# A transformer-like block on one core: three side banks and two maximum banks in PSUM, side work placed by free TensorE time

## The reference

```python
x = x + attn_a(ln(x))   # scores = -|pos_i - pos_j| * scale, causal softmax, 16 heads share it; out @ wo.T + bo
x = x + ffn(ln(x))      # sigmoid(xr W_r) * (relu(xk W_k)**2 W_v), xr and xk mix a token with the one before
x = x + attn_b(ln(x))   # 16 heads of 16 channels, softmax(q k / 4), causal
x = x + ffn(ln(x))      # the same weights as the first one
```

## Time and profile before

| what | us |
|---|---|
| three runs, median (lowest to highest) | 2311.16 (2307.39 to 2319.46) |
| the profiled execution's own time | 2316.06 |
| its span, first to last instruction | 2314.3 |
| PE busy (share of the span) | 1929.1 (83%) |
| DVE busy | 1417.5 (61%) |
| ACT busy | 1254.3 (54%) |
| POOL busy | 1024.2 (44%) |

### The profile page before, as it was taken

The page is one execution under the profiler, slowest core; times in us unless marked ns, Lnnn a source line. Parts: engine busy times, 40 slices in busy tenths (PEclk is TensorE's granted clock), DMA queues, the critical chain, the costliest instruction groups (busy, mean ns, idle before and its releaser), DMA issues. The chain is left out here.

```text
span 2314.3 us, 32515 instructions
## 1 busy us (share of the span) xinstructions
PE 1929.1 (83%) x9842; PEld 936.3 (40%) x9842; DVE 1417.5 (61%) x4173; ACT 1254.3 (54%) x2673; POOL 1024.2 (44%) x1074
## 2 busy tenths in 40 slices
PE   4477888888988899788987889888887889988986
PEld 3344343334433354324543345333443335432423
DVE  2336677567676666666765666756656666677642
ACT  0623654675537555394545755366554855555563
POOL 4454354335642455334743266423654246422414
PEclk8677899989998899989999899998999899999998
DMA  3006011310132111211122011231113111141100
GB/s 96 0 20 117 1 28 42 69 28 15 43 85 34 28 29 53 67 29 28 33 67 64 13 29 37 76 63 28 28 37 83 28 28 28 43 87 29 29 19 19
DMA packets 64347, 97.27 MB, mean 42 GB/s; under 512 B 15655, under 2 KB 58029, under 8 KB 58030
## 3 DMA queue, kind: packets, MB, share of 16 engines
q1 hardware_dynamic: 64174, 95.20, 18.6%
HBM read 61.09 MB, written 33.55 MB: 41 GB/s over the span
## 5 line engine op out<-in xcount | busy, mean ns | idle before, releaser
L852 ACT ACTIVATE pt<-exp_bank 128x512 f32<-128x512 f32 (+3 forms) x1536 | 742.5, 494 | 806.5 <-PE exp_bank L822 797.0
L867 DVE CUSTOM_DVE_ANT_0 max_bank<-max_bank,mask 128x128 f32<-128x128 f32 (+3 forms) x1024 | 500.3, 502 | 495.2 <-PE max_bank L811 478.2
L822 PE MATMUL exp_bank<-qs,ks 98*128 98x512 bf16 (+3 forms) x1536 | 523.8, 347 | 72.5 <-ACT pt L852 66.3
L811 PE MATMUL max_bank<-ks,qs 96*128 96x512 bf16 (+3 forms) x1536 | 525.0, 349 | 24.3 <-DVE piece_max L870 17.2
L870 DVE TENSOR_REDUCE piece_max<-max_bank 128x1 f32<-128x512 f32 x512 | 342.9, 686 | 164.7 <-PE max_bank L811 161.5
L837 PE MATMUL o_bank<-pt,v 128*17 128x512 f32 (+3 forms) x3072 | 346.2, 525 | 8.0 <-ACT pt L852 3.0
L889 POOL TENSOR_SCALAR_AFFINE_SELECT pt<-pt 128x512 f32<-128x512 f32 x256 | 170.1, 664 | 404.2 <-ACT pt L852 403.8
L353 POOL TENSOR_SCALAR xh<-xs,mv,rstd 128x256 f32<-128x256 f32 x256 | 322.6, 1266 | 10.0 <-PE side L379 3.8
L822 PEld LDWEIGHTS exp_bank<-qs,ks 98*128 98x128 bf16 x1536 | 153.9, 101 | 353.4 <-ACT pt L852 229.5
L811 PEld LDWEIGHTS max_bank<-ks,qs 96*128 96x128 bf16 x1536 | 154.7, 101 | 257.9 <-issue 102.1
L544 PE MATMUL side<-vp,p 128*128 128x260 f32 x576 | 185.2, 450 | 33.7 <-ACT p L473 18.3
(11 more groups left out here) (94 smaller groups left out, 2243.0 us busy)
## 6 DMA issues: line engine op xcount, KB each, us to landing
parts_dram<-parts SPq DMA_DIRECT2D x64, 384.0 KB, 2.6
qs<-parts_dram SPq DMA_DIRECT2D x192, 128.0 KB, 7.0
ks<-parts_dram SPq DMA_DIRECT2D x32, 384.0 KB, 4.8
xs<-in_L_attn_a_x_dram SPq DMA_DIRECT2D x16, 512.0 KB, 4.3
ks<-parts_dram SPq DMA_DIRECT2D x32, 256.0 KB, 5.5
out_dram<-xs SPq DMA_DIRECT2D x16, 512.0 KB, 3.1
ks<-parts_dram SPq DMA_DIRECT2D x32, 128.0 KB, 5.9
qs<-neg_maxT SPq DMA_DIRECT2D x64, 8.0 KB, 1.9
```

Source lines behind the costliest of these rows:

```text
L811: pe.matmul(max_bank[u % MAX_BANKS][:, 0:k1 - k0], qs[r][0:KROWS, j, P * tile:P * (tile + 1)], ks[r][0:KROWS, j, k0:k1], start=True, stop= ...
L822: pe.matmul(exp_bank[k % EXP_BANKS][:, 0:q1 - q0], ks[r][:, j, P * kt:P * (kt + 1)], qs[r][:, j, q0:q1], start=True, stop=True).then_inc(s ...
L852: act.activation(pt[:, e % 2, j, 0:q1 - q0], exp_bank[k % EXP_BANKS][:, 0:q1 - q0], ACT.Exp, scale=SCALE).then_inc(exp_done, 1)
L867: dve.tensor_tensor_reduce(scores, scores, mask[:, HALF - w:HALF], 1.0, LOWEST, ALU.add, ALU.max, piece_max[:, j, m:m + 1]).then_inc(max_f ...
```

## The change

Eight PSUM banks are divided anew: `side` gets three, `max_bank` two, `exp_bank` keeps two, `o_bank` one. `place()` no longer counts in quarters but in **ticks**. A tick is one side part. `LEFT[u]` is what 2700 columns of PE time leave when the attention of quarter u has had its own (300 at least); the ticks of a group's 48 quarters are shared out in proportion to it, so that 48 ticks still span 48 quarters. `moment(tick)` turns a tick into a quarter with a fraction; the fraction keeps several ticks in one quarter in order, and `schedule()` lists side steps by it. Worked through for the 12 pieces of a group, a quarter gets between 1.06 and 1.46 ticks where it has no products with v, and between 0.19 and 0.65 where it has them (0.19 where both matmuls and the products are at or near 512 columns). The starts, lags and due times of the stages are changed as well, and the long functions of the first attention on PE, DVE and ACT are cut into several generators, so that their steps may be listed interleaved (their semaphores stay as they were). The set-up at the start still uses two side banks in turn.

```diff
-MAX_BANKS, EXP_BANKS = 3, 2
+MAX_BANKS, EXP_BANKS = 2, 2
...
-ATT1, FFN2, FFN4, PROJ3 = -44, 50, 82, 114
-FIRST = {("att1", 0): -220, ("ffn2", 0): -126, ("proj3", 0): -74,
-         ("att1", 1): -28, ("ffn2", 1): 66, ("proj3", 1): 114}
+ATT1, FFN2, FFN4, PROJ3 = -46, 35, 75, 112
+FIRST = {("att1", 0): -240, ("ffn2", 0): -154, ("proj3", 0): -88,
+         ("att1", 1): -36, ("ffn2", 1): 50, ("proj3", 1): 112}
...
-LN_HALF = {"att1": 8, "ffn2": 16, "ffn4": 16, "proj3": 12}
+LN_HALF = {"att1": 12, "ffn2": 20, "ffn4": 20, "proj3": 10}
...
-PIECE_TIME = [2 + (q1 - q0) // P for _, q0, q1 in KEY_PIECES] + [5, 5, 5]
-PIECE_AT = [34 + sum(PIECE_TIME[:p]) for p in range(NP + 4)]
+PIECE_TIME = [max(3, 1 + 5 * (q1 - q0) // HALF) for _, q0, q1 in KEY_PIECES] + [5, 5, 5]
+PIECE_AT = [32 + sum(PIECE_TIME[:p]) for p in range(NP + 4)]
...
-        "att1": [("values1", t, 16 + t + TPH * (t // TPH), 1, 1, 2) for t in range(NT)] +
-                [("positions", k, 29 + k, 1, 1, 1) for k in range(6)] +
+        "att1": [("values1", t, 16 + 2 * t + TPH * (t // TPH), 1, 1, 2) for t in range(NT)] +
+                [("positions", k, 26 + k + 7 * (k // 3), 1, 1, 1) for k in range(6)] +
...
-        "ffn": [("keys", j, 24 + 2 * j, 2, 1, 1) for j in range(2)] +
-               [("receptance", j, 31 + 2 * j, 2, 1, 1) for j in range(2)] +
-               [("products", j, 36 + 2 * j, 2, 1, 2) for j in range(2)],
-        "proj3": [("project", j, 24 + 3 * j, 2, 1, 1) for j in range(8)] +
-                 [("values3", j, 26 + 6 * j, 2, 3, 2) for j in range(4)]}
+        "ffn": [("keys", j, 24 + 3 * j, 2, 1, 1) for j in range(2)] +
+               [("receptance", j, 30 + 4 * j, 2, 1, 1) for j in range(2)] +
+               [("products", j, 37 + 3 * j, 2, 1, 2) for j in range(2)],
+        "proj3": [("project", j, 24 + 4 * j, 2, 1, 1) for j in range(8)] +
+                 [("values3", j, 26 + 4 * j, 2, 1, 2) for j in range(4)]}
...
+def attention_time(u):
+    t, j = divmod(u, GH)
+    width = [k1 - k0 for _, k0, k1 in QUERY_PIECES][t % NP] + [q1 - q0 for _, q0, q1 in KEY_PIECES][(t - LEAD) % NP]
+    return width + (4 * ([q1 - q0 for _, q0, q1 in KEY_PIECES][(t - LEAD - 1) % NP] + 64) if j == GH - 1 else 0)
+
+LEFT = [max(2700 - attention_time(u), 300) for u in range(GH * NP)]
+TICK = [0]
+for u in range(QUARTERS + 200):
+    TICK.append(TICK[-1] + LEFT[u % (GH * NP)] * GH * NP / sum(LEFT))
...
-    free, before, shift, u = [BEGIN, BEGIN], BEGIN, 0, BEGIN
+    free, before, shift, tick = [BEGIN, BEGIN, BEGIN], BEGIN, 0, BEGIN
...
-        side = [psum(f"side{k}") for k in range(2)]
+        side = [psum(f"side{k}") for k in range(3)]
...
-                for entry in parts:
-                    while entry[0] <= u:
-                        entry[0] = next(entry[1], NEVER)
-                parts = [entry for entry in parts if entry[0] < NEVER]
+                while parts and (first := min(parts, key=lambda entry: entry[0]))[0] < u + 1:
+                    first[0] = max(first[0], next(first[1], NEVER))
+                    if first[0] == NEVER:
+                        parts.remove(first)
```

More of the change, by code:

```diff
@@ L116, in stage_jobs, with moment @@
     return jobs
+def attention_time(u):
[6 more added lines that the diff above has]
+    TICK.append(TICK[-1] + LEFT[u % (GH * NP)] * GH * NP / sum(LEFT))
+def moment(tick):
+    if tick < 0:
+        return tick
+    u = next(u for u, at in enumerate(TICK) if at >= tick - 1e-6)
+    first = next(k for k in range(tick, -2, -1) if k < 0 or u > 0 and TICK[u - 1] >= k - 1e-6)
+    return u + (tick - first - 1) / 8
 def place():
@@ L130, in place @@
     quarters, bank, emptied, late = {}, {}, {}, []
-    free, before, shift, u = [BEGIN, BEGIN], BEGIN, 0, BEGIN
+    free, before, shift, tick = [BEGIN, BEGIN, BEGIN], BEGIN, 0, BEGIN
     while parts or rows:
-        while rows and rows[0][0] <= u and min(free) <= u:
+        u = moment(tick)
+        while rows and rows[0][0] <= u and min(free) <= tick:
             key = rows.pop(0)[1]
             k = free.index(min(free))
-            quarters[key], bank[key], emptied[key] = [u], k, u + 2
-            free[k] = u + 2
+            quarters[key], bank[key], emptied[key] = [u], k, moment(tick + 2)
+            free[k] = tick + 2
         if parts:
@@ L140, in place @@
             regained = max(0, shift - max(0, at - before) // 4)
-            if at + regained <= u and (k > 0 or min(free) <= u):
+            if at + regained <= tick and (k > 0 or min(free) <= tick):
                 parts.pop(0)
-                before, shift = at, max(regained, u - at)
+                before, shift = at, max(regained, tick - at)
                 late.append((at, shift))
@@ L150, in place @@
                 if last:
-                    emptied[key] = free[bank[key]] = u + delay[key]
-        u += 1
+                    free[bank[key]] = tick + delay[key]
+                    emptied[key] = moment(tick + delay[key])
+        tick += 1
     return quarters, bank, emptied, late
@@ L159 @@
 BANK[0,], BANK[1,] = 0, 1
-END = max(EMPTIED_AT.values()) + 20
+END = int(max(EMPTIED_AT.values())) + 20
 WRITTEN_AT = {}
@@ L381, in pe_transposed, with dve_values1 @@
                 mm.then_inc(tr_full, 1)
-        def dve_att1(at, n):
+        def dve_values1(n):
             dve = nc.vector
-            def values(t):
+            for t in range(NT):
+                yield EMPTIED_AT["values1", "att1", n, 0, t]
                 dve.wait_ge(v1_full, 8 * n + t + 1)
@@ L407, in distance, with dve_residuals @@
                                          op0=ALU.max, op1=ALU.add).then_inc(dist2_ready, 1)
-            def residual(t):
+        def dve_residuals(n):
+            dve = nc.vector
+            for t in range(NT):
+                yield EMPTIED_AT["attend", "att1", n, 0, t]
                 bank = side_of("attend", "att1", n, 0, t)
@@ L416, in residual, with act_positions, act_distances @@
                                          op0=ALU.mult, op1=ALU.add).then_inc(x1_done, 1)
[L418 to L433, removed]
-            act = nc.scalar
[L436 to L440, removed]
+        def act_positions(n):
+            for k in range(6):
+                h, c = divmod(k, 3)
+                yield EMPTIED_AT["positions", "att1", n, 0, k]
+                nc.scalar.wait_ge(pb_full, 6 * n + k + 1)
+                nc.scalar.activation(pb[:, c, HALF * h:HALF * (h + 1)], side_of("positions", "att1", n, 0, k)[:, :],
+                                     ACT.Copy).then_inc(pb_ready, 1)
+        def act_distances(at, n):
+            act = nc.scalar
             def square(p, c):
@@ L506, in pool_att1, with pe_values1 @@
                                        sq[:, p % 2, 1, 0:w], ALU.add).then_inc(sum_ready, 1)
-        def pe_att1(n):
+        def pe_values1(n):
             pe = nc.tensor
-            def values(t):
+            for t in range(NT):
+                job = "values1", "att1", n, 0, t
+                yield PARTS_AT[job][0]
                 if t % TPH == 0:
                     pe.wait_ge(xt_ready, 2 * LN_AT["att1", n, t // TPH] + 2)
-                bank = side_job(("values1", "att1", n, 0, t), vp_ready, 8 * n + t + 1)
+                bank = side_job(job, vp_ready, 8 * n + t + 1)
                 for c in range(NC):
@@ L518, in values, with pe_positions @@
                 mm.then_inc(v1_full, 1)
-            def positions(c, h):
+        def pe_positions(n):
+            pe = nc.tensor
+            for k in range(6):
+                h, c = divmod(k, 3)
+                job = "positions", "att1", n, 0, k
+                yield PARTS_AT[job][0]
                 pe.wait_ge(vp_ready, 8 * n + TPH * (h + 1))
-                bank = side_job(("positions", "att1", n, 0, 3 * h + c), pb_ready, 6 * n + 3 * h + c + 1)
+                bank = side_job(job, pb_ready, 6 * n + k + 1)
                 for t in range(TPH):
@@ L527, in positions, with pe_attend @@
                 mm.then_inc(pb_full, 1)
+        def pe_attend(n):
+            pe = nc.tensor
             for t in range(NT):
[L530 to L536, removed]
+                job = "attend", "att1", n, 0, t
+                yield PARTS_AT[job][0]
                 m = t + 1 if t < TPH else TPH + t + 1
@@ L781, in sp_stack @@
                 copy(qs[r], 1, slot, part, 1)
-        emptied = [None, None]
+        emptied = [None, None, None]
         def side_of(*job):
```

56 lines of the change are left out of this document (29 added, 27 removed).

## The result

The changed kernel takes **2178.5 us** (median of 4 runs, 2177.5 to 2179.3) against 2311.7 us: a ratio of 0.942, 95% interval 0.9395 to 0.9446. The prediction was 2216 us in a range of 2150 to 2320: the sign and the range held, the size was too small by 38 us. The experiments show, however, that the reasons I gave were only in part the right ones.

The account below looks back on a forecast made before the run. PE sets the pace, with 22.0 of 37.5 idle us per turn in side-bank waits. Per turn -15 + 6 + 0 - 5 = -14 us; 6.6 turns give -92, last stretch -3: 2216 us, range 2150 to 2320.

Parts of the forecast that it names:

- The term of the third bank: PE's side jobs: third bank, wider spacing and even quarters remove two thirds of 22.0 us bank waits, -15 us per turn.
- The ring of two: PE's maximum matmul waits for DVE's reduction with two maximum banks: +6 us per turn, ends 0 and +20.
- Distances: First attention's pieces spaced over 56 ticks instead of 60, ACT full there: 0 us per turn, ends -4 and +8.
- The clock: Denser PE work in the turn gives part of the granted clock back: -5 us per turn, ends -16 and +5.
- The moved dates: Later stores and earlier due times in the turn: stack and x loads still fit, both 0.
- Start-up, last stretch, tail: Start-up and tail wait for data: 0, with +-10 us; last stretch has few side jobs: -3 us.
- rival 1: More than forecast: bank waits -20, clock -8, maximum ring +4 per turn, about 2150 us; chance 0.12.
- rival 2: Third bank worth little, evictions stand behind reductions and exponentials: -3 us per turn, about 2290 us; chance 0.22.
- rival 4: The granted clock falls and the kernel is slower; its sign is a clock under 0.90; chance 0.05.
- rival 5: ACT: denser distances cost +8, bank waits -10, ring +4, clock -2: no change, about 2310 us; chance 0.05.
- rival 3: Two-bank maximum ring binds where DVE is busiest, stopping PE and ACT: +15 us per turn, about 2410 us; chance 0.08.
- The signs: Changed profile: turn 259 us, PE idle about 25, side waits 7, L811 6 to 10, exp waits near 8, clock 0.95 to 0.96.

Follow-up runs that it names:

- banks-only: Kernel before with three side banks and two maximum banks, equal quarters and dates of before: 2158.2 us, ratio 0.933.
- best kernel: Changed kernel (three side, two maximum banks, ticks) with the starts, lags, piece times and due times of the kernel before: 2145.0 us, ratio 0.9293.
- order-only kernel: Changed kernel's ticks and dates with the banks of before (two side, three maximum): 2335.6 us, ratio 1.0091.

## Why the prediction was right, and where not

- *What bounds the kernel.* Right: PE sets the pace, and the waits for side banks were what could go. Taking the banks alone removed them and gave 6.7%.
- *The term of the third bank, -15 us per turn.* Near in size, for a reason that was half wrong. The lines of the 22.0 us gave 16.4 in the changed kernel (to 5.6) and 17.6 in the banks-only one (to 4.4), which kept the equal quarters. So the discount to two thirds for bursts had no ground, and "even quarters" added nothing that shows. (The 22.0 also left out 1.1 us at L544 and 1.1 at L644, which wait for evictions too.) I had misread the wait of the earlier trace rows. Between the two reductions and L958 the trace has the line below.

```profile
1215.57 0.69 DVE L870 TENSOR_REDUCE piece_max<-max_bank 128x1 f32<-128x512 f32 x1 [0.51 <-PE max_bank L811]
```

DVE was not behind: it stood idle for 0.51 us, and L954 and L958 were listed after the reduction of a maximum that PE had issued only at 1215.03. PE waited for a step that stood behind PE's own latest matmul. That a late eviction still makes it when the bank is asked for one job later fits the banks-only run.

- *The ring of two, +6 us.* The mechanism is right, and so is the nearest row, but the waits became 12.5 us, thus +10.1. I had the exp waits at 0, and they gave back 4.9 (8.6 to 3.7). That the two errors nearly cancel is luck. The time depends on the order: 14 us under the old one, all in the last stretch, and 57 under the new.
- *Distances.* 0 us, right: taken back in the changed kernel they give nothing (0.9417 against 0.942).
- *The clock, -5 us.* Too small: busy time fell by 7.8 us per turn, at a clock of 0.95 instead of 0.94, and by 13.5 in the banks-only kernel, at 0.98. That denser PE work gives clock back was my estimate from the order of the windows in the earlier trace rows; no run shows it by itself.
- *The moved dates.* This is the step that failed. I had costed them by the SP queue and the distances alone, put late inputs of the side jobs at nothing, and counted the wider spacing among what helps. The new dates cost about 30 us. In the turn shown, L564, L405 and L534 idle 7.6 us, 5.7 of it for data; with the dates of before they idle 3.2, 0.7 of it for data.
- *Start-up, last stretch, tail.* -2.4, -1.2 and -1.4 us against 0, -3 and 0. Right within the 10 us.
- *The sum.* -14 per turn against -20.4 measured. The 6.4 us are 1.4 at the side lines, -4.1 at the ring, 4.9 at the exp waits, 1.4 at other lines and 2.8 of busy time. In 6.6 turns they are 42 us, about the 38 by which the prediction was off, and rival 1 (2150) was nearer than the forecast. Rivals 2, 4 and 5 fell; rival 3's mechanism is in the trace, at a third of its price.
- *The signs.* Idle time (24.9 us for 25) and clock (0.95) came as said. The maximum's matmul waits 12.5 us, above the 6 to 10, and the exp waits are 3.7, not near 8.
- *The clock and the ring of two (rival 4, 0.05).* No run shows a ground for the fall to which I gave 0.05: the changed kernel's turn has 0.95, and none of the turns shown is under 0.92, where rival 4's sign was under 0.90. Under the new order with two side banks the ring of two took the turn's clock from 0.95 to 0.92 and made its busy time 8.3 us longer, which is the direction of rival 4. Under the old order the clock went from 0.94 to 0.93, less than two turns of the banks-only kernel differ (0.98 and 0.96). What the ring of two takes from the clock beside the third bank, no run shows.

## What to carry to other kernels

When one resource is enlarged and a long order is re-tuned in the same change, run the resource alone first: here it gave 6.7%, and the new order took a part of it back. Count PSUM banks by what waits for them: a bank moved from a ring that waited 2.4 us per turn to one that cost 22.0 added 4.6 us of waits to the first and brought the second's down to 4.4. Price a ring together with the waits behind it in the same loop and with the clock, in the order that it will meet. When due dates move, count late inputs as well as full buffers.

## What was not expected of the hardware

**Busy time is no constant.** The same 9842 matmul instructions kept PE busy for 1929.1, 1863.6 and (best kernel) 1852.5 us. In the banks-only kernel's steady part the busy time gave 70.0 us beside 79.8 of idle time, at a clock of 0.97 instead of 0.94. But less idle time alone doesn't explain a higher clock: the order-only kernel idles more than the kernel before (435.7 us against 385.2) and is busy for less (1902.8 us), with 0.95 in its steady part.

**Equal stretches, another clock.** In the last stretch the banks-only kernel and the best one are alike in PE's waits for the maximum banks (19.8 and 18.8 us), but not in clock. Three windows of 20 us in the profile of the first, then three of the second at the same place in the work:

```profile
1861.30:1881.30 20.00, 17.47 (x82) 6.22 (x82) 16.55 (x30) 8.56 (x19) 6.53 (x7) 0.79 0.38 106
...
1901.30:1921.30 20.00, 17.39 (x96) 5.08 (x92) 15.81 (x35) 11.15 (x25) 3.85 (x6) 0.82 0.47 80
...
1941.30:1961.30 20.00, 18.21 (x88) 4.86 (x88) 14.34 (x35) 9.15 (x22) 3.89 (x6) 0.67 0.44 80
```

```profile
1859.60:1879.60 20.00, 17.16 (x95) 5.82 (x93) 17.14 (x36) 9.28 (x21) 6.29 (x7) 0.91 0.40 106
...
1899.60:1919.60 20.00, 16.95 (x107) 5.21 (x106) 15.36 (x35) 12.42 (x28) 3.26 (x5) 1.00 0.38 55
...
1939.60:1959.60 20.00, 17.24 (x108) 5.38 (x106) 16.79 (x48) 12.24 (x27) 4.44 (x7) 1.00 0.14 23
```

The whole stretch takes 238.3 us at 0.90 in the one and 220.5 at 0.98 in the other. Both fall to 0.50 in the first window, after PE had thinned out: it was busy for 3.5 of 6 us (1868 to 1874) in the first and for 1.7 of 4 (1866 to 1870) in the second. Then the first stays at 0.50 from 1873 to about 1883, the second only from 1871 to about 1874, both with PE busy nearly all of that time. After that the first falls again and the second hardly does (0.84 from 1883 us and 0.99 from 1874 us), at like busy shares (0.84 to 0.91, until about 2001 us). Nothing in these rows tells why. That profile is the slowest of its four runs (2168.5 us; the others 2154.8 to 2160.7), and its 18 us are more than what the ticks seem to give. How much of the ticks' 9 us is order and how much is this clock stays open.
